# Reordering the engine queues of a fused linear-attention and FFN kernel: weight preparations, x's upper part, the last tiles' masks and y's parts

## The chip, the cores and the metric

The kernel runs on one core of one Trainium2 chip. The metric is the device time of one execution in microseconds (us). "PE" is TensorE, "DVE" VectorE, "ACT" ScalarE, "POOL" GpSimd and "SP" SyncE, whose queue starts every DMA of this kernel.

## What is computed

```python
x = L0_attn_x                                  # (8, 1024, 512) f32
x = x + attn(layernorm(x), W_attn, b_attn, W_proj, b_proj)
x = x + ffn(layernorm(x), weight, bias)
# attn: q, k, v = split(x @ W_attn + b_attn), 16 heads of 32
#       q, k = elu(q) + 1, elu(k) + 1
#       kv += k v^T; ksum += k, token by token (causal, linear attention)
#       y = (q kv) / (q ksum + 1e-6);  out = y @ W_proj + b_proj
# ffn:  e4m3(x) @ e4m3(weight).T + bias, operands rounded to fp8
```

## The kernel before

The 8192 tokens are cut into NT = 64 tiles of 128. Every engine runs its own hand-written list of steps in one loop over the tile number n, and semaphores alone tie the lists together; within a list nothing overtakes. So the order in which a helper is called in an engine's loop is the order in its queue, and a step whose semaphore is late holds all that stands behind it.

The work of tile n: TensorE makes the causal scores of two halves (`scores(n)`), VectorE multiplies them by a mask into `raw` (also called `scores(n)` on its list, "the mask" below), TensorE multiplies them, the queries and the running state by v (`values(n)`), VectorE divides (`values(n)`: `den`, then `y`). y is split into two f16 parts (ACT the upper, POOL the lower) and transposed by a DMA into `yt`. For the last four tiles (`tail(n)`, n = 60 to 63) TensorE transposes y (`t_y`), ACT copies the upper part (`s_yth`) and VectorE subtracts the lower one (`s_ytl`). One tile later TensorE projects (`proj(n)`: 12 matmuls, of which the last four alone read y's lower part), VectorE adds the result to x and takes the statistics of the second layer norm; POOL normalises (`proj(n)` on its list, into `x2`), ACT rounds to fp8 and bf16 (`t2`), a DMA transposes (`x2t`; for tiles 62 and 63 TensorE), and in the tile after that TensorE runs `ffn(n)`; ACT takes the result out (`o16`), VectorE adds it (`ffn`), and SP stores the rows.

For four tiles at a time TensorE makes twelve products ahead: eight "features" (q and k; `phi` on ACT and DVE turns each into `qk`) and four v. `chunks(n)` spreads them over the loop, three in each tile, the third behind the step `k_tokens`. The last tiles have none left. Products and transposes share four PSUM banks in a ring (`take`): the k-th waits until the (k-4)-th is emptied. `update(n)` on TensorE and VectorE moves the running state (`mid`, `state`), `spread` on ACT copies it into v, `queries` copies q (`raw<-qk`). `ln1` is the first layer norm eight tiles ahead: its upper f16 part is made by ACT and its lower by POOL (`ln1_parts`, `xnhl`), and SP starts a transposing DMA into `xt`.

W_proj is split into `wph` and `wpl` (`proj_weight`), the FFN weight is clipped and rounded to fp8 in steps (`ffn_low`, `ffn_high`, `ffn_round`, `ffn_sum`). SP's loop over n holds, in this order: the transposing of y(n-1), of x2(n-2), of x(n+8), in n = 1 the four of the FFN weight, the load of tile n+10 (for tiles 10 to 13 behind `s_wpl`, since their buffer holds W_proj first), and the store of tile n-2, which waits for VectorE's `ffn(n-2)`.

ACT's loop, which sets the steps of the tail, has this order:

```python
if n >= 2:
    t2(n - 2)
ahead(chunks(n)[0])
if tail(n - 1):
    t_y(n - 1)
if n + 1 < NT:
    k_tokens(n + 1)
```

Of the kernel before, what the change touches and what calls it, by code (L numbers as in the profile page):

```python
# [20 lines left out]
NT = B * T // P  # L21
# [4 lines left out]
NX = 14  # L26
# [23 lines left out]
def tail(n):  # L50
    return n >= NT - 4


def chunks(n):


    j, c = divmod(n, 4)
    if n < NT - 5:
        return [(j + 1, 3 * c), (j + 1, 3 * c + 1)], [(j + 1, 3 * c + 2)]
    return [(NB - 1, 9 + n - (NT - 5))] if n < NT - 2 else [], []  # L60
# [15 lines left out]
def build(nc, x_d, wa_d, ba_d, wp_d, bp_d, wf_d, bf_d, out_d):  # L76
    ctx = ExitStack()
    with ctx:
# [9 lines left out]
        xs = sb("xs", [P, NX, D], F32)  # L88
# [35 lines left out]
        st2 = sb("st2", [P, 4, 12], F32)  # L124
# [79 lines left out]
        def _(e):  # L204
# [13 lines left out]
            def matmul(out, a, b, start, stop):  # L218
                return e.matmul(out, a, b, start=start, stop=stop, skip_group_check=True)  # L219
# [116 lines left out]
            def proj(n):  # L336
                out = take(("proj", n), s_x1, n + 1)
                pe.wait_ge(s_wpl, 1)
                if tail(n):
                    pe.wait_ge(s_yth, n - NT + 5)  # L340
                    pe.wait_ge(s_ytl, n - NT + 5)
                else:
                    pe.wait_ge(s_yt[n % 2], 16 * (n // 2 + 1))
                mms = [(a + h, b, h) for a, b in ((0, wph), (0, wpl), (4, wph)) for h in range(4)]
                for i, (k, b, h) in enumerate(mms):
                    mm = matmul(out[:, :], yt[:, n % 2, k, :], b[:, h, :], i == 0, i == 11)
                mm.then_inc(s_proj, 1)

# [56 lines left out]
        def _(e):  # L405
# [45 lines left out]
            def ln1_parts(m):  # L451
                act.wait_ge(s_xn, m + 1)
                if m >= 8:
                    act.wait_ge(s_xt[m % 4], 16 * (m // 4 - 1))
                copy(xnhl[:, m % 4, 0, :], xn[:, m % 2, :]).then_inc(s_xhi, 1)
# [73 lines left out]
            def ahead(made):  # L529
                for j, s in made:  # L530
                    if s < 8:
                        phi(j, ORDER[s])
# [33 lines left out]
            for n in range(NT + 2):  # L566
                j, c = divmod(n, 4)
                if n < NT:
                    if n == 0:
                        spread(n)  # L570
                        proj_weight()
# [4 lines that stand above are left out]
                        t_y(n - 1)  # L576
                    if n + 1 < NT:
                        k_tokens(n + 1)
                    if n + 8 < NT:
                        ln1_parts(n + 8)  # L580
                    if n:
                        ahead(chunks(n)[1])
                    if n + 1 < NT:
                        queries(n + 1)
                    values(n)
                    if n == 0:
                        ahead(chunks(n)[1])
                if n == NT - 1:
                    t_y(n)
                if n >= NT:  # L590
                    t2(n - 2)
                if n >= 2:
                    ffn(n - 2)
                if n + 1 < NT:
                    spread(n + 1)

        @block.vector
        def _(e):
            dve = Engine(e)

            def stats(src, row, s_bn, s_var, n):
                e.bn_stats(row[:, 0:6], src).then_inc(s_bn, 1)  # L602
                dve.wait_ge(s_bn, 2 * n + 1)
                e.bn_aggr(row[:, 6:8], row[:, 0:6]).then_inc(s_bn, 1)  # L604
                dve.wait_ge(s_bn, 2 * n + 2)
                e.tensor_scalar(row[:, 8:9], row[:, 6:7], -1.0, None, ALU.mult)
                e.tensor_scalar(row[:, 9:10], row[:, 7:8], LN_EPS, None, ALU.add).then_inc(s_var, 1)  # L607
# [75 lines left out]
            def proj(n):  # L683
                x = xs[:, n % NX, :]
                dve.wait_ge(s_proj, n + 1)
                dve.wait_ge(s_xb, xb_count(n))
                e.scalar_tensor_tensor(x, bank["proj", n][:, :], UN_P, x, ALU.mult, ALU.add).then_inc(s_x1, 1)  # L687
                dve.wait_ge(s_x1, n + 1)
                if n >= 4:
                    dve.wait_ge(s_x2, n - 3)  # L690
                stats(x, st2[:, n % 4, :], s_bn2, s_var2, n)

            def ffn(n):
                x = xs[:, n % NX, :]
# [4 lines left out]
            def ahead(made):  # L699
                for j, s in made:  # L700
                    if s < 8:
                        phi(j, ORDER[s])
                    else:
                        v_out(j, s - 8)
# [72 lines left out]
            def ffn_high():  # L777

                dve.wait_ge(s_whi, 1)
                dve.wait_ge(s_wfd, 1)  # L780
                e.scalar_tensor_tensor(w_hi, w_hi, 2.0, w_lo, ALU.mult, ALU.subtract, saturate=False).then_inc(s_wfd, 1)
# [6 lines left out]
            def ffn_sum(first, end):  # L788
                dve.wait_ge(s_wfd, 3)
                for f in range(first, end):  # L790
                    e.tensor_tensor(w_b[:, f, :], w_hi[:, f, :], w_lo[:, f, :], ALU.add).then_inc(s_wfd, 1)
# [36 lines left out]
            update(0)  # L828
            proj_scale()
            for n in range(NT + 2):  # L830
                j, c = divmod(n, 4)
                if n < NT:
                    scores(n)
                    if n == 1:
                        ffn_sum(0, 2)
                    if n + 8 < NT:
                        ln1(n + 8)
                    if n == 0:
                        ffn_high()
                    ahead(chunks(n)[0][:1])  # L840
                    ahead(chunks(n)[0][1:])
                    if tail(n - 1):
                        t_y(n - 1)
                    if n:
                        ahead(chunks(n)[1])
                    values(n)
                    if n == 0:
                        ahead(chunks(n)[1])
                if 1 <= n <= NT:
                    proj(n - 1)  # L850
                if n + 1 < NT:
                    update(n + 1)
                if n == 0:
                    proj_weight()
                    ffn_round()
                if n == 1:
                    ffn_sum(2, 4)
                if n == NT - 1:
                    t_y(n)
                if n >= 2:  # L860
                    ffn(n - 2)

        @block.gpsimd
        def _(e):
# [80 lines left out]
            for n in range(NT + 1):  # L945
                if n < NT:
                    if n + 8 < NT:
                        ln1(n + 8)
                    if n + 8 < NT:
                        add_bp(n + 8)  # L950
                        ln1_parts(n + 8)
                    if n < 8:
                        add_bp(n)
                    values(n)
                if n >= 1:
                    proj(n - 1)
# [105 lines left out]
```

## Time and profile before

| | us |
|---|---|
| median of 3 runs (lowest to highest) | 989.68 (987.88 to 990.79) |
| profiled execution, its own time | 989.57 |
| span in the profile | 987.8 |
| TensorE busy | 951.9 (96%) |
| VectorE / ScalarE / GpSimd busy | 703.1 / 743.6 / 503.9 |
| mean granted TensorE clock | 0.990 |

The span runs from the first to the last instruction; 1.8 us of the execution's own time lie outside it. A granted clock of 1.00 is 2.4 GHz, 0.50 is 1.2 GHz. Busy time tells which engine is close to full; the waits tell where it stands still.

### The profile page before, as it was taken

To read this page: it belongs to the slowest core of one execution; us is meant where nothing else is said; L and a number is where in the kernel's file an instruction comes from. 1 tells how busy PE (TensorE), PEld (TensorE's weight loads), DVE (VectorE), ACT (ScalarE), POOL (GpSimd) and SP (SyncE) were. 2 spreads that over 40 slices of the span, in tenths; PEclk is the share of its full clock that TensorE was granted. 3 is DMA by queue.
4 is the path that set the end of the run, shared out by engine and by line. 5 is a ranking of instruction groups with operands and counts; after the bars stand their busy time and mean duration, and the time that the engine had idled before them with its cause. 6 is when DMAs were issued, how large, how long until landed. Compare 5 with 4: busy or idle time off the path is not lost.

```text
span 987.8 us, 44710 instructions
## 1 busy us (share of the span) xinstructions
PE 951.9 (96%) x19698; PEld 521.7 (53%) x19760; DVE 703.1 (71%) x1395; ACT 743.6 (75%) x1423; POOL 503.9 (51%) x521
## 2 busy tenths in 40 slices
PE   5998999999999999999999999999999999999985
PEld 2454555555555555555555555555555555555552
DVE  6977777676676777668677677767667676765674
ACT  5776686877878688787868868687786868777763
POOL 5536656555555455464555555555545546432323
PEclk9999999999999999999999999999999999999998
DMA  8824454544454434434335345454354453422311
GB/s 267 127 35 83 77 99 72 83 93 73 83 92 85 86 77 93 74 81 95 76 83 93 72 79 97 72 83 93 83 79 86 92 79 77 84 45 56 57 35 48
DMA packets 185362, 82.58 MB, mean 84 GB/s; under 512 B 165841, under 2 KB 165841, under 8 KB 185169
## 3 DMA queue, kind: packets, MB, share of 16 engines
q1 hardware_dynamic: 185168, 79.73, 42.6%
q8 instruction: 155, 2.54, 1.1%
q14 instruction: 39, 0.31, 0.1%
HBM read 22.81 MB, written 16.78 MB: 40 GB/s over the span
## 4 chain that ended last, share of the span: by engine, by line
PE 92%; DVE 4%; issue 1%; ACT 1%; POOL 1%; DMA 0%; POOLq 0%
PE R L219 76%; PE S L219 13%; PE R L223 3%; DVE raw L641 1%; POOL st L868 1%; DVE st L602 1%; POOL xn L870 0%; DVE xs L687 0%; DVE xs L697 0%; DMA xs<-in_L_attn_x 0%; ACT raw L409 0%; DVE v L630 0%; DVE wpl L769 0%; ACT wl L428 0%; DVE st L604 0%
## 5 line engine op out<-in xcount | busy, mean ns | idle before, releaser
L219 PE MATMUL R<-xt,wh 128*128 128x512 f16 x1024 | 306.8, 382 | 3.0 <-ACT wh L409 2.4
L409 ACT ACTIVATE raw<-qk 64x512 f32<-64x512 f32 x256 | 160.8, 628 | 76.8 <-PE S L219 73.8
L618 DVE SCALAR_TENSOR_TENSOR qk<-qk,rel 128x512 f32<-128x512 f32 x128 | 98.0, 768 | 149.8 <-ACT rel L421 145.3
L899 POOL TENSOR_TENSOR yhl<-y,yhl 128x512 f16<-128x512 f32 x60 | 69.5, 1159 | 255.8 <-ACT yhl L409 255.8
L219 PE MATMUL R<-xt,wl 128*128 128x512 f16 x512 | 194.2, 380 | 0.0
L868 POOL TENSOR_TENSOR st<-st,half 128x1 f32<-128x1 f32 x128 | 74.8, 584 | 168.3 <-DVE st L607 166.9
L219 PE MATMUL R<-wh,xt 128*128 128x512 f16 x512 | 160.3, 379 | 0.0
L641 DVE TENSOR_TENSOR raw<-S,causal 64x1024 f32<-64x1024 f32 x128 | 155.9, 1218 | 0.9
L219 PEld LDWEIGHTS R<-xt,wh 128*128 128x128 f16 x1024 | 96.8, 98 | 110.7 <-DVE xt L735 2.6
L418 ACT ACTIVATE qk<-R,bqk,wm 128x512 f32<-128x512 f32 x128 | 98.9, 772 | 61.4 <-PE R L219 61.3
L219 PE MATMUL R<-wph,yt 128*128 128x512 f16 x512 | 134.2, 385 | 2.0 <-DVE yt L680 2.0
L630 DVE SCALAR_TENSOR_TENSOR v<-R,wm,bv 64x512 f32<-64x512 f32 x128 | 96.0, 750 | 25.9 <-PE R L219 24.0
L421 ACT ACTIVATE rel<-R,bqk,wm 128x512 f32<-128x512 f32 x128 | 98.6, 770 | 2.3 <-DVE qk L618 2.3
L219 PEld LDWEIGHTS S<-v,raw 128*32 128x32 f32 x8192 | 79.3, 110 | 33.9 <-issue 26.5
L219 PE MATMUL R<-wl,xt 128*128 128x512 f16 x256 | 97.0, 379 | 0.0
L219 PE MATMUL S<-v,raw 128*32 128x33 f32 x8192 | 86.7, 199 | 7.8 <-DVE raw L641 5.9
L602 DVE BATCH_NORM_STATS2 st<-xs 128x6 f32<-128x512 f32 x128 | 88.8, 694 | 6.3 <-DMA xs<-in_L_attn_x 2.3
L687 DVE SCALAR_TENSOR_TENSOR xs<-R,wm,xs 128x512 f32<-128x512 f32 x64 | 48.0, 750 | 63.5 <-PE R L219 63.5
L885 POOL TENSOR_TENSOR xnhl<-xn,xnhl 128x512 f16<-128x512 f32 x60 | 70.1, 1169 | 29.4 <-ACT xnhl L409 29.4
L908 POOL TENSOR_TENSOR xs<-xs,bf 128x512 f32<-128x512 f32 x64 | 82.0, 1281 | 5.3
L892 POOL TENSOR_TENSOR xs<-xs,bp 128x512 f32<-128x512 f32 x64 | 82.2, 1284 | 4.7
L409 ACT ACTIVATE v<-mid 32x132 f32<-32x132 f32 x256 | 80.3, 314 | 3.8 <-DVE mid L652 0.9
(88 smaller groups left out, 1330.0 us busy)
## 6 DMA issues: line engine op xcount, KB each, us to landing
xs<-in_L_attn_x SPq DMA_DIRECT2D x64, 256.0 KB, 3.7
out<-xs SPq DMA_DIRECT2D x64, 256.0 KB, 2.3
raw<-in_L_attn_W_attn SPq DMA_DIRECT2D x3, 1024.0 KB, 10.6
xs<-in_L_attn_W_proj SPq DMA_DIRECT2D x4, 256.0 KB
raw<-in_L_ffn_weight SPq DMA_DIRECT2D x1, 1024.0 KB, 17.6
x2t<-x2b SPq DMA_TRANSPOSE x62, 2.4
xt<-xnhl SPq DMA_TRANSPOSE x60, 4.1
yt<-yhl SPq DMA_TRANSPOSE x60, 3.3
```

Source lines behind the costliest of these rows:

```text
L219: return e.matmul(out, a, b, start=start, stop=stop, skip_group_check=True)
L409: return e.activation(out, in_, ACT.Copy, **more)
L418: e.activation(dst[:, i, :], bank["qkv", j, i][:, :], ACT.Exp, scale=UN[i // 4], bias=bqk[:, i:i + 1])
L421: e.activation(rel[:, u % 2, :], bank["qkv", j, i][:, :], ACT.Relu, scale=UN[i // 4], bias=bqk[:, i:i + 1]).then_inc(s_relu, 1)
L602: e.bn_stats(row[:, 0:6], src).then_inc(s_bn, 1)
L618: e.scalar_tensor_tensor(qk[j % 2][:, i, :], qk[j % 2][:, i, :], 1.0, rel[:, (u - 1) % 2, :], ALU.min, ALU.add).then_inc(s_phi, 1)
L630: made = e.scalar_tensor_tensor(v1[rows, n % NV, a, :, 0:32], heads(bank["qkv", j, 8 + t][rows, :]), UN_V[rows], heads(bv[rows, :]), ALU.m ...
L641: made = e.tensor_tensor(dst, scored(a), causal_over(a), ALU.mult)
L868: e.tensor_tensor(row[:, 10:11], row[:, 9:10], half[:, :], ALU.pow).then_inc(s_rs, 1)
L885: e.tensor_tensor(xnhl[:, m % 4, 1, :], xn[:, m % 2, :], xnhl[:, m % 4, 0, :], ALU.subtract).then_inc(s_xlo, 1)
L892: e.tensor_tensor(x, x, bp[:, :], ALU.add).then_inc(s_xb, 1)
L908: e.tensor_tensor(x, x, bf[:, :], ALU.add).then_inc(s_x1b, 1)
```

## The change

Nothing is computed differently; instructions change places in three queues, and one wait moves.

- VectorE: `proj_weight` (wpl) goes ahead of tile 0's features, `ffn_high` and `ffn_round` behind tile 0's y; `ffn_sum(0, 2)` behind `ln1(9)`. The statistics of the second layer norm become a step of their own (`ln2`). For tiles 58 to 61 they, and `ffn` of the tile before, are called one iteration later, behind the mask of tiles 60 to 63. In n = 63 `t_y(63)` comes ahead of `ln2(62)`.
- ScalarE: x's upper part (`ln1_parts`) is made behind the third product of the tile instead of ahead of it. GpSimd: `add_bp(n)` of the first eight tiles goes ahead of `ln1_parts(n + 8)`.
- TensorE: in the tail's `proj` the wait for y's lower part stands ahead of the ninth matmul instead of the first.

```diff
 def proj(n):                       # TensorE
     if tail(n):
         pe.wait_ge(s_yth, n - NT + 5)
-        pe.wait_ge(s_ytl, n - NT + 5)
...
     for i, (k, b, h) in enumerate(mms):
+        if tail(n) and i == 8:
+            pe.wait_ge(s_ytl, n - NT + 5)
         mm = matmul(out[:, :], yt[:, n % 2, k, :], b[:, h, :], i == 0, i == 11)
...
 # ScalarE's loop
         k_tokens(n + 1)
-    if n + 8 < NT:
-        ln1_parts(n + 8)
     if n:
         ahead(chunks(n)[1])
+        if n + 8 < NT:
+            ln1_parts(n + 8)
...
     if n == 0:
         ahead(chunks(n)[1])
+        ln1_parts(n + 8)
...
 # VectorE
     e.scalar_tensor_tensor(x, bank["proj", n][:, :], UN_P, x, ALU.mult, ALU.add).then_inc(s_x1, 1)
+
+def ln2(n):
     dve.wait_ge(s_x1, n + 1)
     if n >= 4:
         dve.wait_ge(s_x2, n - 3)
-    stats(x, st2[:, n % 4, :], s_bn2, s_var2, n)
+    stats(xs[:, n % NX, :], st2[:, n % 4, :], s_bn2, s_var2, n)
...
         scores(n)
+        if tail(n):
+
+            ln2(n - 2)
+            ffn(n - 3)
...
     if 1 <= n <= NT:
         proj(n - 1)
+    if n == NT - 1:
+        t_y(n)
+    if 1 <= n <= NT and not NT - 4 <= n + 1 < NT:
+        ln2(n - 1)
     if n + 1 < NT:
         update(n + 1)
-    if n == 0:
-        proj_weight()
-        ffn_round()
...
-    if n >= 2:
+    if n >= 2 and not NT - 4 <= n + 1 < NT:
         ffn(n - 2)
...
 # GpSimd's loop
         add_bp(n + 8)
-        ln1_parts(n + 8)
     if n < 8:
         add_bp(n)
+    if n + 8 < NT:
+        ln1_parts(n + 8)
```

VectorE's queue from tile 0's `ln1(8)` to the mask of tile 1, before (`wpl<-xs` is `proj_weight`; `raw<-raw` with 2048 elements is `ffn_high`, then `ffn_round`; `raw<-S` the mask). Line numbers of the changed kernel are two to four higher for the same step.

```order
L781 SCALAR_TENSOR_TENSOR raw<-raw 128x2048
L618 SCALAR_TENSOR_TENSOR qk1<-qk1,rel 128x512 x2
L666 TENSOR_SCALAR den<-S 128x16
L668 RECIPROCAL den<-den 128x16
L676 TENSOR_TENSOR y<-S,den 128x512
L618 SCALAR_TENSOR_TENSOR qk1<-qk1,rel 128x512
L652 TENSOR_TENSOR mid<-R3,state 128x132
L655 TENSOR_TENSOR state<-R0,mid 128x132
L769 SCALAR_TENSOR_TENSOR wpl<-xs,wm,wph 128x2048
L785 TENSOR_SCALAR raw<-raw 128x2048
L641 TENSOR_TENSOR raw<-S,causal 64x4x256 x2
```

The same stretch of VectorE's queue in the changed kernel:

```order
L773 SCALAR_TENSOR_TENSOR wpl<-xs,wm,wph 128x2048
L620 SCALAR_TENSOR_TENSOR qk1<-qk1,rel 128x512 x2
L668 TENSOR_SCALAR den<-S 128x16
L670 RECIPROCAL den<-den 128x16
L678 TENSOR_TENSOR y<-S,den 128x512
L785 SCALAR_TENSOR_TENSOR raw<-raw 128x2048
L789 TENSOR_SCALAR raw<-raw 128x2048
L620 SCALAR_TENSOR_TENSOR qk1<-qk1,rel 128x512
L654 TENSOR_TENSOR mid<-R3,state 128x132
L657 TENSOR_TENSOR state<-R0,mid 128x132
L643 TENSOR_TENSOR raw<-S,causal 64x4x256 x2
```

wpl has taken the place of `ffn_high`, and both steps on the FFN weight stand between y(0) and tile 0's third feature; nothing of the weights is left between `state` and tile 1's mask.

VectorE's queue in the tail, from proj(58)'s addition to x (`xs<-R3`) to v of the next tiles, before (`st2` are the statistics of tile 58, `xs<-o16` is ffn(57), `raw<-S` the mask of tile 60):

```order
L687 SCALAR_TENSOR_TENSOR xs<-R3,wm,xs 128x512
L602 BN_STATS st2<-xs 128x6
L604 BN_AGGR st2<-st2 128x2
L606 TENSOR_SCALAR st2<-st2 128x1
L607 TENSOR_SCALAR st2<-st2 128x1
L652 TENSOR_TENSOR mid<-R1,state 128x132
L655 TENSOR_TENSOR state<-R2,mid 128x132
L697 TENSOR_TENSOR xs<-o16,xs 128x512
L641 TENSOR_TENSOR raw<-S,causal 64x4x256 x2
L630 SCALAR_TENSOR_TENSOR v1<-R3,wm,bv 64x16x32 x2
```

The same stretch in the changed kernel:

```order
L689 SCALAR_TENSOR_TENSOR xs<-R3,wm,xs 128x512
L654 TENSOR_TENSOR mid<-R1,state 128x132
L657 TENSOR_TENSOR state<-R2,mid 128x132
L643 TENSOR_TENSOR raw<-S,causal 64x4x256 x2
L604 BN_STATS st2<-xs 128x6
L606 BN_AGGR st2<-st2 128x2
L608 TENSOR_SCALAR st2<-st2 128x1
L609 TENSOR_SCALAR st2<-st2 128x1
L701 TENSOR_TENSOR xs<-o16,xs 128x512
L632 SCALAR_TENSOR_TENSOR v1<-R3,wm,bv 64x16x32 x2
```

The mask has gone from behind the statistics and ffn to ahead of both; the same happens in the next three tiles.

ScalarE's queue in n = 62, which reads the same before and after (`x28`, `x2b` are t2(60), made of POOL's normalised tile 60; `yt` is the upper part of y(61), `ktok` belongs to update(63), `raw<-qk1` are the queries of tile 63):

```order
L410 ACTIVATE x28<-x2 128x512
L410 ACTIVATE x2b<-x28 128x512
L410 ACTIVATE yt<-R0 128x512
L410 ACTIVATE ktok<-R1 128x512
L410 ACTIVATE raw<-qk1 64x2x256 x4
```

Nothing moved there: t2(60) still stands ahead of the upper part of y(61).

## Rows read from the trace of the kernel before

**Rows 1.** TensorE's waits from 50 us on (us in total, times, longest)

```profile
PE S L219 <- DVE raw L641: 5.9, 3, 2.5
PE S L219 <- DVE y L676: 3.8, 1, 3.8
...
PE S L219 <- issue: 1.9, 1, 1.9
...
PE R L219 <- ACT rel L421: 0.6, 1, 0.6
```

**Rows 2.** Windows, a steady one and one behind a long wait (busy, PEclk)

```profile
500.00:600.00 100.00, 99.50 (x2133) 54.50 (x2138) 72.31 (x144) 76.39 (x151) 52.89 (x54) 1.00 0.46 83
...
82.00:86.00 4.00, 3.88 (x73) 2.17 (x74) 3.86 (x11) 3.54 (x10) 2.75 (x3) 0.63 0.89 110
```

**Rows 3.** Timeline of VectorE, 57 to 74 us (start, us, line, op)

```profile
57.18 2.28 DVE L781 SCALAR_TENSOR_TENSOR raw<-raw 128x2048 fp8e4<-128x2048 fp8e4 x1
...
66.57 0.69 DVE L618 SCALAR_TENSOR_TENSOR qk<-qk,rel 128x512 f32<-128x512 f32 x1 [4.68 <-ACT rel L421]
...
67.71 2.34 DVE L769 SCALAR_TENSOR_TENSOR wpl<-xs,wm,wph 128x2048 f16<-128x2048 f32 x1
69.97 1.22 DVE L785 TENSOR_SCALAR raw<-raw 128x2048 fp8e4<-128x2048 fp8e4 x1
```

**Rows 4.** Timeline of TensorE, 70 to 84 us

```profile
73.61 1.30 PE L219 MATMUL S<-v,raw 128*32 128x33 f32 x128 [1.23 <-DVE raw L641]
...
82.12 1.28 PE L219 MATMUL S<-qk 32*64 32x64 f32 x64 [3.83 <-DVE y L676]
```

**Rows 5.** Timeline of GpSimd and SP's queue, 57 to 71 us

```profile
57.35 2.52 POOL L868 TENSOR_TENSOR st<-st,half 128x1 f32<-128x1 f32 x1 [13.51 <-DVE st L607]
...
65.28 1.16 POOL L899 TENSOR_TENSOR yhl<-y,yhl 128x512 f16<-128x512 f32 x1 [0.27 <-ACT yhl L409]
...
70.48 1.24 SPq L982 DMA_TRANSPOSE yt<-yhl  x1
```

**Rows 6.** SP's queue, yt's landing times (915 us on) and TensorE, tile 60

```profile
928.81 0.34 SPq L1036 DMA_DIRECT2D out<-xs  x1
929.24 1.29 SPq L982 DMA_TRANSPOSE yt<-yhl  x1
...
DMA to landing us min/median/max: 3.0/4.0/5.0
...
934.66 1.69 PE L219 MATMUL R<-wph,yt 128*128 128x512 f16 x4
```

**Rows 7.** Timeline of VectorE, GpSimd and ScalarE, tiles 60 to 62

```profile
950.58 0.69 DVE L602 BATCH_NORM_STATS2 st<-xs 128x6 f32<-128x512 f32 x1
...
952.79 2.45 DVE L641 TENSOR_TENSOR raw<-S,causal 64x1024 f32<-64x1024 f32 x2
...
951.82 0.55 POOL L868 TENSOR_TENSOR st<-st,half 128x1 f32<-128x1 f32 x1 [7.60 <-DVE st L607]
952.47 1.04 POOL L870 TENSOR_SCALAR x<-xs,st 128x512 f32<-128x512 f32 x1
...
953.89 0.63 ACT L409 ACTIVATE x<-x 128x512 fp8e4<-128x512 f32 x1
...
955.09 0.58 ACT L409 ACTIVATE yt<-R 128x512 f16<-128x512 f32 x1
```

**Rows 8.** Timeline of TensorE, tiles 61 to 63 and the end

```profile
947.01 1.02 PE L219 MATMUL R<-wph,yt 128*128 128x512 f16 x4 [0.58 <-DVE yt L680]
...
951.24 0.91 PE L219 MATMUL S<-qk 32*64 32x64 f32 x64
...
961.91 0.91 PE L219 MATMUL S<-qk 32*64 32x64 f32 x64
...
971.03 0.60 PE L223 MATMUL R<-ident,y 128*128 128x128 f32 x4
...
980.29 0.63 PE L223 MATMUL R<-ident,x 128*128 128x128 f32 x4 [0.81 <-POOL x L870]
```

More of the change, by code:

```diff
@@ L830, in _ @@
             for n in range(NT + 2):
-                j, c = divmod(n, 4)
                 if n < NT:
                     scores(n)
-                    if n == 1:
-                        ffn_sum(0, 2)
+                    if tail(n):
+                        ln2(n - 2)
+                        ffn(n - 3)
                     if n + 8 < NT:
@@ L838, in _ @@
                     if n == 0:
-                        ffn_high()
-                    ahead(chunks(n)[0][:1])
-                    ahead(chunks(n)[0][1:])
+                        proj_weight()
+                    if n == 1:
+                        ffn_sum(0, 2)
+                    ahead(chunks(n)[0])
                     if tail(n - 1):
@@ L847, in _ @@
                     if n == 0:
+                        ffn_high()
+                        ffn_round()
                         ahead(chunks(n)[1])
@@ L850, in _ @@
                     proj(n - 1)
+                if n == NT - 1:
+                    t_y(n)
+                if 1 <= n <= NT and not NT - 4 <= n + 1 < NT:
+                    ln2(n - 1)
                 if n + 1 < NT:
                     update(n + 1)
-                if n == 0:
-                    proj_weight()
-                    ffn_round()
                 if n == 1:
                     ffn_sum(2, 4)
-                if n == NT - 1:
-                    t_y(n)
-                if n >= 2:
+                if n >= 2 and not NT - 4 <= n + 1 < NT:
                     ffn(n - 2)
```

## The prediction, made before the changed kernel ran

> **What bounds the kernel now.** I read the busy time by stretches first. In the steady part TensorE is busy for 99.5 of 100 us at the full clock [rows 2], with VectorE and ScalarE below 77 and GpSimd at 53. There an order is worth something only if it makes TensorE wait. Then the list of TensorE's waits from 50 us on [rows 1]: three waits for the mask (5.9 us), one for y (3.8), one for a feature (0.6), and 1.9 us put down to "issue". In the timeline they lie at two places: at tiles 0 to 2, and in the last four tiles, where no products made ahead fill the gaps. So two places are costed; the 57 tiles between are asked only whether they stay hidden. The granted clock is 0.63 in the 4 us from scores(2) on, which follow the 3.8 us wait [rows 2, 4]; the reader is to see that a long wait is paid for twice.
>
> **The head: what goes.** VectorE stands idle for 4.68 us between y(0) and tile 0's third feature, because ScalarE holds that feature back behind x's upper part and the queries; right behind it come wpl (2.34 us) and ffn_round (1.22), and only then the mask of tile 1 [rows 3]. The change puts wpl where ffn_high was (2.34 against 2.28 us, no matter) and ffn_high and ffn_round (2.28 + 1.22 = 3.5 us) into the idle 4.68. ScalarE's feature also comes about 0.6 us earlier. So tile 1's mask comes some 4.6 us earlier, and the 0.6 us wait for the feature [rows 1] and the 1.23 us wait for tile 1's mask, ahead of its values [rows 4], are gone. y(1) also loses x(9)'s path through VectorE, GpSimd and ScalarE ahead of its last feature, so it gains more, about 7 us; scores(2) moves up only by TensorE's own three waits, 0.6 + 1.2 + 3.8 = 5.7 us (to about 76.4, y(1) being ready near 75), and the slow clock behind the long wait goes with it: 4.0 us at 0.63 lose at most 1.5 us, I take 1.4. That is -7.1 us.
>
> **The head: what comes.** GpSimd's tiny power op took 2.52 us at 57.35, while VectorE ran ffn_high from 57.18 to 59.46 [rows 3, 5]; the same op takes 0.55 elsewhere [rows 7]. So ffn_high, in its new place, holds GpSimd for up to 2.3 us, and ffn_round perhaps for another 1.2, at 62 to 65.5 us, where GpSimd now has two additions of the projection's bias, x(8)'s lower part (itself later, since its upper part is made some 3 us later) and then y(0)'s lower part, which ended at 66.44 before. Undisturbed I put it at 67.1, held for the full 3.5 us at 70.3. SP issued y(0)'s transposing at 70.48 although y was ready 4 us before: it stood behind the load of tile 10, which waits for wpl; that wait is over at 59.5 now. proj(0) began 1.2 us behind the start of the values at 73.61 [rows 4], so it will want yt at 74.8 - 0.6 - 1.2 = 73.0. Undisturbed, issue at 67.7 and a landing of 3.0 to 5.0 us [rows 6] give at the latest 72.7: no wait. Held for 3.5 us, issue at 70.9 gives 73.9 to 75.9: 0.9 to 2.9 us. I take 1.2 us; bounds 0 and 2.9. The Trainium skill (GPSIMD Engine Reference, section 8, Key points) says that GpSimd shares its SBUF interfaces with VectorE and contends with VectorE's instructions that have two SBUF inputs or run in a 2-port mode. The trace agrees for ffn_high; whether the one-input ffn_round counts no row shows. If it does in full, this term would be about 2.0 instead of 1.2 by that page, if the page did not hold at all, 0. The head comes to -7.1 + 1.2 = -5.9 us (-7.1 to -4.2).
>
> **The middle: nothing.** ScalarE's later upper part of x delays x's transposing by 2 to 3 us in two tiles of four; it is made eight tiles ahead, and in the two tiles whose third product is v the order is as before. GpSimd's lower part of x then ends well before y's, for which it waits anyway. If that cover failed, TensorE would wait at each group of four tiles; nothing in 99.5 of 100 us points to it.
>
> **The tail, tile 60.** SP's store of tile 57 waits for VectorE's ffn(57), and the transposing of y(59) stands right behind it (928.81, 929.24 [rows 6]). ffn(57) now comes behind the mask (2.45 us) and the statistics (1.2): SP is released 3.5 us later, at 932.7 for y(59). With the 4.0 us landing of the row proj(59) can begin at 936.8, against 934.66: +2.1 (landing 3.0 to 5.0: +1.1 to +3.1). The 1.9 us of "issue" lie just ahead of 934.66, within tile 60's values; they lie under the new wait, so their absence would give nothing back.
>
> **The tail, tiles 61 to 63.** Let T be the start of scores(n) on TensorE. Before, T advances by 961.91 - 951.24 = 10.7 us a tile [rows 8]. In the changed kernel the chain is: scores 0.9, then the mask 2.45, then the statistics of tile n-2 and GpSimd's normalising, 950.58 to 953.51 = 2.9 us, then ScalarE's t2(n-2) and, right behind it, the upper part of y(n-1), 953.89 to 955.67 = 1.8 [rows 7]; with the handovers proj(n-1) begins at T + 8.3. TensorE has nothing else: its next instruction is that proj. Before, the statistics were two steps ahead of the mask, and y's copy was there in time. From proj to the next scores are 951.24 - 947.01 = 4.2 us at full clock [rows 8]; behind a wait of 2.5 us or more I add the same 1.4 for the slow clock (0 to 1.5); behind the 1.9 us pause four matmuls took 1.69 us, without a wait of that length 1.02 [rows 6, 8]. T advances by 8.3 + 4.2 + 1.4 = 13.9, that is +3.3 us, for 61 to 62 and for 62 to 63. From scores(63) to t_y(63) it was 971.03 - 961.91 = 9.1; now 8.3 + 2.7 + 1.4 = 12.4: +3.3. What the earlier mask saves (0.6 us a tile, since the mask then waits for scores itself) is inside: values run earlier, and then TensorE waits at proj. The ninth matmul's later wait is worth nothing here: y's lower part is 0.7 us behind the upper, and eight matmuls take 1.7.
>
> **The end.** With t_y(63) ahead of the statistics, and proj free to begin on y's upper part, proj(63) begins about 1.4 us earlier after its transposes. But the last transposes of x (980.29 [rows 8], 9.3 us behind t_y(63)) also wait for tile 62 to pass: transposes 0.6, copy 0.6, y's lower part 0.7, statistics and normalising 2.9, transposes 0.6, two copies 1.3, ffn 1.0, handovers 0.4: 8.1 us. That is -1.2.
>
> The tail: +2.1 + 3.3 + 3.3 + 3.3 - 1.2 = +10.8 us. **The sum:** -5.9 + 10.8 = +4.9 on the profiled execution's own 989.57 us, so 994.5; the median of the runs shown, 989.68, is 0.1 away, which changes nothing.
>
> **Rivals.** (A) Forecast: 994.5, chance 0.50. (B) The clock keeps its level through the new waits and GpSimd is not held: head -7.1, tail 10.8 - 3 x 1.4 = 6.6, so 989.1, within 0.3%. For it: after the 1.23 us wait 128 small matmuls took only 1.30 us [rows 4]; against it: the new waits are longer than that, and behind 1.9 and 3.8 us the matmuls were slow [rows 2, 6]. With halfway cases 0.26. (C) Faster: t2(n-2) is not what y's copy stands behind. Then each mask is 0.6 us earlier, the slow stretches of tiles 62 and 63 go (1.4 each), the end gives 1.2: tail -(1.2 + 2.8 + 1.2) = -5.2, head -7.1, 977.3. It is decided by one thing: whether normalised tile n-2 reaches ScalarE before the transposed y(n-1) does; the queue puts it first, and the statistics come 4 us later than they did, so I give it 0.08. (D) Worse: GpSimd's full hold and a slow stretch behind it (head -4.2 + 1.4 = -2.8), a landing of 5.0 us (tail 11.8), and the "issue" pause falling on a bare stretch (1.9 + 1.4): 989.57 - 2.8 + 11.8 + 3.3 = 1001.9; with halfway cases 0.16.
>
> **Numbers.** What a measurement of this kernel can tell from no change is 0.3%, 3.0 us: 986.7 to 992.7. Faster is C, 0.08. Within 0.3% is B, 0.26. Slower is A and D, 0.66. The range takes in the bounds of the head, the landing and the clock: from -7.1 + 6.6 (989.1, cut at 989.0) to -4.2 + 11.8 and one slow stretch of 1.4 more (998.6, cut at 998.5).
>
> **What would show it.** Right: scores(2) at 76 to 78 us; a wait of 0 to 3 us at proj(0); a wait of about 2 us or more for yt at proj(59), with SP's y(59) behind its store; three waits of TensorE for ScalarE's yt in tiles 61 to 63, the clock at half behind them, scores 13 to 14 us apart; t_y(63) to the end about 1 us shorter. Wrong: masks of tiles 62 and 63 still what TensorE waits for, or ScalarE's copies of y where they were.

## The result: 1.2% slower, and why the sum missed it

The changed kernel took 1001.55 us (median of 4 runs, 998.51 to 1002.24) against 990.05 (987.88 to 990.79) before: a ratio of 1.0123, 95% interval 1.0103 to 1.0143. The prediction was 994.5 us with a range of 989.0 to 998.5. The direction was right; the size was not, and the time lies outside the range. Executions of one kernel differ by about 2 us with the granted clock: of the 44 runs of the kernel before that the experiments were set beside, the 16 with a mean clock of 0.993 or more took 987.2 us in the mean and the others 989.4.

The profile after: a span of 1000.5 us, a mean granted clock of 0.987. TensorE's waits from 50 us on, the counterpart of [rows 1]:

```profile
PE R L219 <- ACT yt L410: 9.9, 3, 3.7
PE R L219 <- DMA yt<-yhl: 7.1, 3, 3.5
PE S L219 <- DVE raw L643: 3.5, 2, 2.0
...
PE S L219 <- issue: 1.4, 2, 1.0
```

The three waits of the tail for ScalarE's yt were forecast. Of the 7.1 us for transposed y, 3.2 lie at proj(59), as forecast, 0.3 at proj(0), and 3.5 at a place that the prediction doesn't mention: proj(1).

To see where the time goes I set the start of each scores(n) on TensorE beside that of the kernel before. scores(0) comes 0.7 us later already, ahead of anything that was changed, so the head is counted from there.

| | after minus before, us | forecast |
|---|---|---|
| scores(0) | +0.72 | |
| scores(2), against scores(0) | -4.6 | -5.7 |
| scores(3), against scores(0) | -0.4 | -5.9 |
| scores(3) to scores(60) | +1.0 | 0 |
| scores(60) to (61), to (62), to (63) | +3.1, +3.7, +3.2 | +2.1, +3.3, +3.3 |
| scores(63) to t_y(63), and from there to the end | +3.3, -1.8 | +3.3, -1.2 |

The last two lines of the table come to +11.4 (before rounding), forecast +10.8. The head's gain is there at scores(2) and gone one tile later. TensorE at proj(0), scores(2) and proj(1) after the change (columns as in [rows 4]):

```profile
74.44 1.02 PE L219 MATMUL R<-wph,yt 128*128 128x512 f16 x4 [0.33 <-DMA yt<-yhl]
...
78.23 0.91 PE L219 MATMUL S<-qk 32*64 32x64 f32 x64 [0.35 <-DVE y L678]
87.39 1.44 PE L219 MATMUL S<-v,raw 128*32 128x33 f32 x128
92.32 1.02 PE L219 MATMUL R<-wph,yt 128*128 128x512 f16 x4 [3.50 <-DMA yt<-yhl]
93.18 1.56 PE L219 MATMUL R<-wpl,yt 128*128 128x512 f16 x4
94.54 1.91 PE L219 MATMUL R<-wph,yt 128*128 128x512 f16 x4
```

proj(1) could start at 88.8 and waits until 92.3 for y(1); the groups of four matmuls behind it take 1.56 and 1.91 us instead of 1.03, and the granted clock is 0.69 in the window of 92 to 96 us (columns as in [rows 2]; the clock is the third number from the end):

```profile
92.00:96.00 4.00, 3.68 (x12) 1.52 (x13) 0.00 (x0) 0.56 (x1) 1.51 (x2) 0.69 0.57 132
```

Here is proj(1) before, without a wait:

```profile
93.67 1.04 PE L219 MATMUL R<-wph,yt 128*128 128x512 f16 x4
```

SP's queue shows why. First before, then after the change (the wft rows are the four transposes of the FFN weight, the last yt is y(1)):

```profile
80.33 1.23 SPq L974 DMA_TRANSPOSE xt<-xnhl  x1
81.60 5.97 SPq L1030 DMA_TRANSPOSE wft<-raw  x4
87.62 0.58 SPq L967 DMA_DIRECT2D xs<-in_L_attn_x  x1
88.25 1.24 SPq L982 DMA_TRANSPOSE yt<-yhl  x1
```

```profile
70.75 1.24 SPq L990 DMA_TRANSPOSE yt<-yhl  x1
80.47 1.23 SPq L982 DMA_TRANSPOSE xt<-xnhl  x1
81.75 5.20 SPq L1038 DMA_TRANSPOSE wft<-raw  x4
86.99 0.58 SPq L975 DMA_DIRECT2D xs<-in_L_attn_x  x1
87.62 1.23 SPq L990 DMA_TRANSPOSE yt<-yhl  x1
```

y(1) is ready some 4 us earlier (scores(2), which waited for it in both, moved from 82.12 to 78.23), but its transpose is issued only 0.6 us earlier, and TensorE has it 4.7 us after that, at 92.3. Before, it was in time: the trace puts the landing 3.5 us behind the issue, at 88.25 + 3.5 = 91.8, against a proj(1) that began at 93.67, a slack of 1.9 us that no list of waits shows. Now proj(1) could start 4.9 us earlier (88.8), and the landing is 0.5 us later, since the transpose took 1.1 us longer: 4.9 - 1.9 + 0.5 = 3.5 us of wait. Why it took longer is open.

### The profile page after: what moved, and what is told of

The parts are those of the page before. It is cut to its first block, busy times and chain, and to the rows that moved or that the text cites. A ratio compares the mean times of both kernels' runs of the same rounds, so it can differ in the third digit from the quotient of the medians.

```text
span 1000.5 us, 44771 instructions
## 1 busy us (share of the span) xinstructions
PE 958.9 (96%) x19760; PEld 521.7 (52%) x19760; DVE 712.4 (71%) x1395; ACT 740.3 (74%) x1423; POOL 519.4 (52%) x521
## 4 chain that ended last, share of the span: by engine, by line
PE 90%; DVE 4%; issue 2%; POOL 2%; DMA 1%; ACT 1%; SPq 1%; ACTq 0%; POOLq 0%
PE R L219 75%; PE S L219 12%; PE R L223 3%; DVE raw L643 1%; DMA yt<-yhl 1%; POOL st L875 1%; DVE st L604 1%; SPq L1038 0%; POOL xn L877 0%; ACT x L410 0%; POOL x L877 0%; DVE raw L785 0%; DVE qk L620 0%; DMA xs<-in_L_attn_x 0%; ACT yt L410 0%
## 5 line engine op out<-in xcount | busy, mean ns | idle before, releaser
L620 DVE SCALAR_TENSOR_TENSOR qk<-qk,rel 128x512 f32<-128x512 f32 x128 | 104.0, 815 | 140.2 <-ACT rel L422 138.8
L875 POOL TENSOR_TENSOR st<-st,half 128x1 f32<-128x1 f32 x128 | 89.2, 697 | 161.0 <-DVE st L609 160.7
L219 PE MATMUL R<-wph,yt 128*128 128x512 f16 x512 | 137.1, 392 | 17.0 <-ACT yt L410 9.9
L604 DVE BATCH_NORM_STATS2 st<-xs 128x6 f32<-128x512 f32 x128 | 88.8, 694 | 6.4 <-DMA xs<-in_L_attn_x 2.5
L899 POOL TENSOR_TENSOR xs<-xs,bp 128x512 f32<-128x512 f32 x64 | 84.7, 1328 | 4.7
```

The lines of the kernel that those rows point to most:

```text
L620: e.scalar_tensor_tensor(qk[j % 2][:, i, :], qk[j % 2][:, i, :], 1.0, rel[:, (u - 1) % 2, :], ALU.min, ALU.add).then_inc(s_phi, 1)
L875: e.tensor_tensor(row[:, 10:11], row[:, 9:10], half[:, :], ALU.pow).then_inc(s_rs, 1)
L899: e.tensor_tensor(x, x, bp[:, :], ALU.add).then_inc(s_xb, 1)
```

## Why x(9)'s transpose did not come earlier

SP's y(1) stands behind x(9)'s transpose, and that waits for GpSimd. VectorE (first fence) and GpSimd (second), after the change, 62 to 81 us:

```profile
62.59 3.02 DVE L785 SCALAR_TENSOR_TENSOR raw<-raw 128x2048 fp8e4<-128x2048 fp8e4 x1
65.64 2.17 DVE L789 TENSOR_SCALAR raw<-raw 128x2048 fp8e4<-128x2048 fp8e4 x1
67.73 1.64 DVE L620 SCALAR_TENSOR_TENSOR qk<-qk,rel 128x512 f32<-128x512 f32 x1
...
69.82 2.45 DVE L643 TENSOR_TENSOR raw<-S,causal 64x1024 f32<-64x1024 f32 x2
```

```profile
62.17 4.55 POOL L899 TENSOR_TENSOR xs<-xs,bp 128x512 f32<-128x512 f32 x2
66.69 2.13 POOL L892 TENSOR_TENSOR xnhl<-xn,xnhl 128x512 f16<-128x512 f32 x1
68.78 1.60 POOL L906 TENSOR_TENSOR yhl<-y,yhl 128x512 f16<-128x512 f32 x1
73.54 0.93 POOL L875 TENSOR_TENSOR st<-st,half 128x1 f32<-128x1 f32 x1 [3.15 <-DVE st L609]
74.57 1.85 POOL L877 TENSOR_SCALAR xn<-xs,st 128x512 f32<-128x512 f32 x1
76.50 2.82 POOL L899 TENSOR_TENSOR xs<-xs,bp 128x512 f32<-128x512 f32 x2
79.29 1.15 POOL L892 TENSOR_TENSOR xnhl<-xn,xnhl 128x512 f16<-128x512 f32 x1
```

Before, the same steps of VectorE took 2.28, 1.22 and 0.69 us [rows 3], and one addition on GpSimd 1.28. Now both engines are slower: each takes its own time plus the wait for the other's instruction. GpSimd's first addition runs from 62.17 to 63.45; ffn_high, begun at 62.59, gets its 2.28 us behind it and ends at 65.6; the second addition, held meanwhile, ends at 66.7; ffn_round, begun at 65.64, gets its 1.22 us behind that and ends at 67.8; and so on in turn to y(0)'s lower part. Each sum comes out 0.1 to 0.2 us above its row. Had the two engines shared evenly while both were at work, ffn_high would have ended at 67.0 (an estimate from the same lengths), not at 65.6. The Trainium skill (Trainium Architecture — The Big Picture, What this means for kernel authors) calls the port pair that VectorE and GpSimd share "an exclusive lock (not a bandwidth split)"; the trace agrees, and a lock costs both sides. The prediction charged GpSimd alone.

x(9)'s statistics do reach GpSimd 2.5 us earlier (73.54; before 76.03). Then its normalising takes 1.85 us instead of 0.77, and two additions of the bias (2.82) stand ahead of x(9)'s lower part instead of one (1.27): 1.1 + 1.5 = 2.6 us, all of the 2.5. GpSimd's rows before:

```profile
77.07 0.77 POOL L870 TENSOR_SCALAR xn<-xs,st 128x512 f32<-128x512 f32 x1
77.92 1.27 POOL L892 TENSOR_TENSOR xs<-xs,bp 128x512 f32<-128x512 f32 x1
79.14 1.16 POOL L885 TENSOR_TENSOR xnhl<-xn,xnhl 128x512 f16<-128x512 f32 x1
```

## The experiments

"The end's edits" are the later wait for y's lower part in proj(60) to proj(63), and t_y(63) ahead of the statistics of tile 62. scores(0), which lies ahead of every edit, starts between 0.35 us earlier and 0.84 us later than in the profile of before, so profiles are compared from scores(0) on. The medians of the kernel before were 988.5 to 989.2 in these runs and 990.05 in the result above, so a ratio says more than a difference of medians.

**1. The changed kernel with the tail's late statistics put back.**

```diff
         scores(n)
-        if tail(n):
-            ln2(n - 2)
-            ffn(n - 3)
...
-    if 1 <= n <= NT and not NT - 4 <= n + 1 < NT:
+    if 1 <= n <= NT:
         ln2(n - 1)
...
-    if n >= 2 and not NT - 4 <= n + 1 < NT:
+    if n >= 2:
         ffn(n - 2)
```

> The changed kernel with ln2 and ffn of tiles 57 to 61 back where they were on VectorE (the later wait for y's lower part and t_y(63) ahead of the statistics stay). Theory A (the whole loss is the late statistics of the last tiles; the head gives back what it gains): the profile's tail loses its +11.4 us up to scores(63) and t_y(63) but keeps the shorter end, so 988 to 989.5 us, that is the kernel before less 0.4 (head) and 1 to 1.8 (end); no wait of TensorE for ScalarE's yt over 1 us, none for y(59)'s DMA. Rival B (the reordered head, with its 3.5 us wait at proj(1), carries a large part of the loss): 994 us or more.

Measured: 985.66 us, ratio 0.9973 (0.9959 to 0.9987), 2.8 us under its reference, where theory A's terms came to 1.4 to 2.2. All of the loss is in this part. The wait at proj(1) is still there (3.4 us): scores(3) starts 0.7 us earlier, against scores(0), scores(2) 4.6.

**2. The kernel before with the late statistics alone.** It is the opposite edit, with the statistics as a step of their own:

```diff
         scores(n)
+        if tail(n):
+            ln2(n - 2)
+            ffn(n - 3)
```

> The kernel before with only ln2 and ffn of tiles 57 to 61 moved behind the masks of tiles 60 to 63. Theory A: the loss of the tail by itself, +11 to +13 us (1001 to 1003): +3.1 at tile 60, +3.7 and +3.2 for scores 61 to 62 and 62 to 63, +3.3 to t_y(63), without the end's gain. Rival B (the loss needs the head's edits too): under +6 us. The head must read as in the kernel before: scores(2) near 82, no wait at proj(1).

Measured: 1006.9 us, ratio 1.0184 (1.0163 to 1.0204): above the 1003 of theory A, and worse than the changed kernel. TensorE's waits from 50 us on name the lower part of y now:

```profile
PE R L219 <- DVE yt L680: 13.7, 4, 4.4
```

So the ninth matmul's later wait, forecast as worth nothing, pays for part of the late statistics.

**3. The changed kernel with ScalarE's t2(n-2) behind y's upper part and the keys.**

```diff
-    if n >= 2:
+    if n >= 2 and not tail(n - 1):
         t2(n - 2)
...
     if n + 1 < NT:
         k_tokens(n + 1)
+    if tail(n - 1):
+        t2(n - 2)
```

> The changed kernel with ScalarE's t2(n-2) put behind y's upper part and k_tokens in n = 61 to 63. Theory A1 (the queue on ScalarE is what makes proj wait): the three waits for yt (9.9 us) go; proj(n-1) starts at about T + 4.7 to 6, and ffn(n-2) then waits for x2t, which still lands at T + 10 to 12, so scores(61) to scores(62) take about 12.5 us instead of 14.35: 995 to 997 us in all. Rival A2 (the late statistics themselves bind; the order on ScalarE only chooses which matmuls wait): the wait moves whole to ffn(n-2), and no more than 1 us is gained: 1000 to 1001.5.

Measured: 995.95 us, ratio 1.0074 (1.0052 to 1.0096): theory A1. ScalarE no longer stands idle in front of y's copy; x's rounding follows it:

```profile
947.10 0.60 ACT L410 ACTIVATE yt<-R 128x512 f16<-128x512 f32 x1 [1.45 <-PE R L223]
947.60 0.60 ACT L410 ACTIVATE ktok<-R 128x512 f32<-128x512 f32 x1
949.53 0.63 ACT L410 ACTIVATE x<-x 128x512 fp8e4<-128x512 f32 x1 [1.34 <-POOL x L879]
```

In the changed kernel GpSimd's and ScalarE's rows of the same tile are:

```profile
949.68 0.93 POOL L875 TENSOR_TENSOR st<-st,half 128x1 f32<-128x1 f32 x1 [13.38 <-DVE st L609]
950.71 0.77 POOL L877 TENSOR_SCALAR x<-xs,st 128x512 f32<-128x512 f32 x1
...
951.51 0.63 ACT L410 ACTIVATE x<-x 128x512 fp8e4<-128x512 f32 x1 [3.89 <-POOL x L877]
952.17 0.63 ACT L410 ACTIVATE x2b<-x 128x512 bf16<-128x512 fp8e4 x1
952.71 0.58 ACT L410 ACTIVATE yt<-R 128x512 f16<-128x512 f32 x1
```

There ScalarE is idle for 3.89 us, in the last 2.5 of which the transposed y lies ready (its transposes run from 948.45 to 949.05), behind the head of ScalarE's queue. But x2 now comes late to ffn, and TensorE waits there instead, 5.9 us in three waits:

```profile
PE R L219 <- DMA x2t<-x2b: 5.9, 3, 2.9
```

**4. The changed kernel with SP's store of tile 57 behind y(59)'s transpose.**

```diff
     if 1 <= n <= NT:
         t_y(n - 1)
+    if n == NT - 4:
+        store(n - 3)
...
-    if n >= 2:
+    if n >= 2 and n != NT - 5:
         store(n - 2)
```

> The changed kernel with the store of tile 57 behind the transposing of y(59) on SP's queue (one place). Theory A (the store waits for the late ffn(57) and holds y(59)): y(59) is issued at about 929 instead of 934.1, the 3.2 us wait at proj(59) goes, ffn(58) waits up to 2.5 us for x2t(58) instead, and 2 to 3.5 us are gained: 998 to 999.5 us. Rival (y(59) lands late for another reason, or x2t(58) takes all of it over): within 0.5 us of the changed kernel, 1001 to 1002.

Measured: 999.81 us, ratio 1.0115 (1.0095 to 1.0136). The wait at proj(59) is gone, and the twelve matmuls of proj(59) run at the full clock: from scores(60) to (61) 1.4 us are gained on the kernel before, where the changed kernel loses 3.1. The next tile loses 5.4 instead of 3.7, so a part is waited for again. The profile is 3.4 us shorter than the changed kernel's, the medians differ by 1.7, between theory A and the rival, and the two ratios differ by 0.8 us, with intervals that overlap. So the cause of the wait at proj(59) is shown; what its removal is worth in this kernel is not resolved.

**5. The edits of experiments 3 and 4 together.**

> The changed kernel with two moves in the last tiles together: ScalarE's additions to x for t2(n-2) stand behind y's and ktok's work for n = 61, 62 and 63 (alone: 995.95 us), and SP's store of tile 57 stands behind y(59)'s transpose (alone: 999.81). Theory S (the two waits are separate terms of the sum, 9.9 us at proj(60) to proj(62) behind ScalarE and 3.2 us at proj(59) behind the store): the gains add, 992.5 to 994.5 us, with no wait of 1 us or more at proj(59). Rival T (the time saved at proj(59) is waited for again at proj(60), because y(60) hangs on VectorE's chain and not on TensorE): 995 to 996.5 us.

Measured: 992.47 us, ratio 1.0051 (1.0036 to 1.0067). The gains add, theory S, and with 1.7 us to spare: by medians 5.6 and 1.7 us alone, 9.1 together. It is still slower than before: late statistics leave waits for x2t (5.8 us in five).

**6. The first experiment's kernel, with SP's FFN weight transposes split around y(1).** It is the one that tests the head.

```diff
     if 1 <= n <= NT:
         t_y(n - 1)
+    if n == 1:
+        ffn_weight(0, 2)
+    if n == 2:
+        ffn_weight(2, 4)
     if n >= 2:
         t2(n - 2)
     if n + 8 < NT:
         t1(n + 8)
-    if n == 1:
-        for f in range(4):
-            sp.wait_ge(s_wfd, 4 + f)
-            e.dma_start(wft[:, :, f * P:(f + 1) * P], w_b[:, f, :], transpose=True).then_inc(s_wft, 16)
```

> The kernel is the changed one with its last tiles as before (that is the run with the tail put back, 985.66 us), and with SP's transposes of feature(0) split: the first two are issued right behind y(0), ahead of t1(9), the last two right behind y(1)'s transpose. Theory Q (what gives the head's gain back is SP's queue, in which y(1)'s transpose stands behind t1(9) and four transposes of feature(0) that end at 86.6 us, so that y(1) lands about 92 while TensorE is ready for proj(1) at 88.8): y(1)'s transpose is issued at 81 to 83 us, the wait of 3.4 us at proj(1) goes, and with it the slow clock behind it (1 to 1.7 us): 980 to 982 us, scores(3) starts 4 to 5 us earlier than in the run with the tail put back. Rival R (y(1) itself is late, or ffn(0) takes up the wait because the last two transposes of feature(0) are later): a wait of 2 to 3 us at the first layer ffn(0) or at proj(1) stays, and the time is within 1 us of 985.7.

Measured: 978.99 us, ratio 0.9921 (0.9894 to 0.9948), 6.7 us under experiment 1. SP's queue and proj(1) on TensorE:

```profile
74.21 3.23 SPq L999 DMA_TRANSPOSE wft<-raw  x2
80.60 1.23 SPq L978 DMA_TRANSPOSE xt<-xnhl  x1
81.88 0.58 SPq L971 DMA_DIRECT2D xs<-in_L_attn_x  x1
82.50 1.24 SPq L986 DMA_TRANSPOSE yt<-yhl  x1
83.78 2.58 SPq L999 DMA_TRANSPOSE wft<-raw  x2
```

```profile
88.77 1.04 PE L219 MATMUL R<-wph,yt 128*128 128x512 f16 x4
89.64 1.03 PE L219 MATMUL R<-wpl,yt 128*128 128x512 f16 x4
```

No wait at proj(1), no slow group behind it, and x(9)'s transpose still where it was: the place of the four transposes is enough to hold y(1) back. scores(3) starts 5.7 us earlier than before, against scores(0); the forecast for the whole head was 5.9. Theory Q. The time is 1 us under the 980 to 982 that it gave: against experiment 1 scores(3) comes 5.1 us earlier, and the two profiles differ by 2.0 us more at tile 60, where the program is the same: the matmuls of proj(59) take 1.03 us a group here, and 1.33, 1.91 and 1.62 there.

**7. The first experiment's kernel, with GpSimd's `add_bp(n)` back behind `ln1_parts(n + 8)`.** `add_bp(n + 8)` stays ahead of it, as in the kernel before, so one addition of two moves, where the expectation speaks of both.

> The kernel is the changed one with its last tiles as before, and with GpSimd's additions of bp(8) and bp(9) and their two partner rows put back behind ln1_parts(8) and ln1_parts(9). Theory Q (SP's queue behind t1(9) sets y(1)'s landing): x's lower part for tile 9 is ready 1.4 to 2.8 us earlier, SP's whole chain moves with it, and the wait of 3.4 us at proj(1) falls to 1 to 2 us: 983.5 to 984.5 us against the 985.66 of the run with the tail put back. Rival R (the landing of y(1) doesn't hang on GpSimd's order): the wait at proj(1) stays at 3 us or more and the time is within 0.7 us of 985.7.

Measured: 983.64 us, ratio 0.9955 (0.9942 to 0.9968). A miss for theory Q's numbers: the wait at proj(1) is 3.3 us (3.4 in experiment 1). SP issued x(9)'s transpose 1.2 us earlier, against scores(0), but that issue took 1.93 us instead of 1.23, and y(1)'s came only 0.5 earlier and took 0.6 us longer to be used (5.2 us). The profile shows no gain (scores(3) at -0.5 us against -0.7 in experiment 1), the median shows 2.0 us, and the two intervals overlap. Whether this edit is worth anything is open.

**8. The first experiment's kernel, with GpSimd's additions last in n = 0 and 1.**

```diff
-    if n + 8 < NT:
+    if n + 8 < NT and n >= 2:
         add_bp(n + 8)
-    if n < 8:
+    if 2 <= n < 8:
         add_bp(n)
     if n + 8 < NT:
         ln1_parts(n + 8)
     values(n)
+    if n < 2:
+        add_bp(n + 8)
+        add_bp(n)
```

> The kernel is the changed one with its last tiles as before, and for n=0 and n=1 both additions of bp stand last in GpSimd's row, behind ln1_parts(n+8) and behind y's lower part, so that GpSimd has nothing to do beside VectorE's round and ffn_high of tile 0's weights. Theory M (VectorE's and GpSimd's operations lengthen each other when they run together, 3.02 for 2.28, 2.17 for 1.22 and 1.64 for 0.69 us on VectorE): ffn_high falls to about 2.3, the round to 1.2, the feature's part to 0.7 us, mask(1) comes 2 to 2.5 us earlier, t1(9) is issued at 76.5 to 78 and y(1)'s transpose at 83.5 to 85; the wait at proj(1) falls to 0 to 1.5 us: 981 to 983.5 us. Rival N (these operations are long for another reason, for instance what they read): their durations stay within 0.2 us of 3.02, 2.17 and 1.64, and the time within 1.5 us of 984.5.

Measured: 981.35 us, ratio 0.9934 (0.9908 to 0.9959). VectorE's rows:

```profile
62.04 2.28 DVE L785 SCALAR_TENSOR_TENSOR raw<-raw 128x2048 fp8e4<-128x2048 fp8e4 x1
64.35 1.23 DVE L789 TENSOR_SCALAR raw<-raw 128x2048 fp8e4<-128x2048 fp8e4 x1
65.50 1.64 DVE L620 SCALAR_TENSOR_TENSOR qk<-qk,rel 128x512 f32<-128x512 f32 x1
```

The two weight steps have their old lengths. GpSimd has nothing beside ffn_high; x(8)'s lower part begins at 64.73, behind the start of ffn_round, and is the one held, 1.86 us instead of 1.16. The feature starts beside that part and stays at 1.64, against the expected 0.7. So the length follows what GpSimd has already begun, not what VectorE reads, for the one-input ffn_round too. Rival N falls. y(1)'s transpose is issued at 84.17, the wait at proj(1) falls to 2.4 us (0 to 1.5 was expected, since 5.2 us passed from its issue to its use), and scores(3) starts 3.0 us earlier.

**9. Experiments 6 and 8 in one kernel.**

> The kernel is the changed one with its last tiles as before, with SP's transposes of feature(0) split around y(1)'s (alone: 978.99 us) and with both additions of bp last in GpSimd's row for n=0 and n=1 (alone: 981.35 us). Theory M (VectorE and GpSimd lengthen each other's operations around tile 0, and once y(1) is in time VectorE's way to mask(1) sets scores(2) and all behind it): scores(2) starts 5.5 to 6.5 us before that of the kernel before, measured against scores(0), scores(3) 6.5 to 7.5 us before, and the time is 976.5 to 978 us. Rival T (proj(0), that is y(0)'s landing, takes up what VectorE gains): scores(3) stays within 0.5 us of the split alone, and so does the time, 978.5 to 979.5 us.

Measured: 978.27 us, ratio 0.9897 (0.9880 to 0.9914). It is the fastest version found, 1.0% under the kernel before. scores(2) starts 5.9 us earlier, as expected; scores(3) only 6.2 (6.5 to 7.5 was expected), 0.4 more than in experiment 6, as rival T had it, and the two medians can't be told apart. Theory M's gain at scores(2) is there, and its gain in time is not. From 74 to 106 us TensorE waits for nothing longer than 0.33 us, so there is little left to win in that stretch.

**10. The kernel before with the end's edits alone.**

```diff
         pe.wait_ge(s_yth, n - NT + 5)
-        pe.wait_ge(s_ytl, n - NT + 5)
...
+        if tail(n) and i == 8:
+            pe.wait_ge(s_ytl, n - NT + 5)
...
+    if n == NT - 1:
+        t_y(n)
     if 1 <= n <= NT:
         ln2(n - 1)
```

> The kernel is the one before with two small parts of the change alone: TensorE waits for the lower part of y ahead of the ninth matmul of proj(60) to proj(63) instead of ahead of the first, and VectorE writes the parts of y(63) ahead of the statistics of tile 62. Theory E (the prediction's term for the end, 1.2 us, where the run with the tail put back showed an end that is 1.6 us shorter): 1.0 to 1.8 us are gained behind t_y(63) and none ahead of it, 986.9 to 987.7 us against 988.5. Rival W (the ninth matmul's later wait gains at proj(60) to proj(62) in the order of before too): 1.5 to 3 us more, 984 to 985.5 us.

Measured: 985.56 us, ratio 0.9969 (0.9958 to 0.9980): 3.6 us under its reference, near rival W. The waits of 0.58 us [rows 8] and 1.43 us for VectorE's yt are gone; 0.6 us are gained from scores(61) to scores(62) and 1.8 behind t_y(63). The profile gains another 1.3 us from scores(62) to scores(63), where the 2.1 us wait for a mask has no slow group behind it (1.43 us in the first fence, 1.96 before in the second, both for the same 128 matmuls), and 2.0 at tile 60. These two can't be put down to the edits: experiment 7 has the same steps in its last tiles and took 1.99 us there, and the edits begin only behind tile 60's matmuls. So the waits alone are worth about 2.4 of the 3.6 us:

```profile
953.45 1.43 PE L219 MATMUL S<-v,raw 128*32 128x33 f32 x128 [2.12 <-DVE raw L642]
954.82 1.04 PE L219 MATMUL R<-wph,yt 128*128 128x512 f16 x4
```

```profile
955.29 1.96 PE L219 MATMUL S<-v,raw 128*32 128x33 f32 x128 [2.11 <-DVE raw L641]
957.18 1.82 PE L219 MATMUL R<-wph,yt 128*128 128x512 f16 x4
```

**11. The changed kernel with the wait for y's lower part ahead of the first matmul again.**

> The changed kernel with one part undone: TensorE waits for the lower part of y ahead of the first matmul of proj(60) to proj(63) again, instead of ahead of the ninth. Theory L (behind the late statistics the upper part of y is the last thing that proj waits for, and the lower part comes 0.7 to 1.2 us after it, so that the later wait hides it in three or four tiles): proj waits for the lower part, 4.4 us each for three tiles, and the time is 2 to 4.5 us over the changed kernel's 1001.55, 1003.5 to 1006 us. Rival N (the later wait is worth nothing there, as forecast): within 1 us of 1001.55.

Measured: 1004.46 us, ratio 1.0160 (1.0143 to 1.0177), 2.9 us over the changed kernel. proj waits for the lower part for 3.4, 4.4 and 4.4 us, then 0.64 at proj(63). Theory L.

## Why the prediction was wrong

**The head: what goes: nearly right.** The waits for tile 0's feature and tile 1's mask are gone, the one for y is 0.35 us (forecast 0). scores(2) came at 78.23 us, outside the 76.4 that the text gave and just beyond its 76 to 78, since 0.33 us of wait at proj(0), 0.36 for `mid` and 0.35 for y were left, 1.0 of the 5.7, and scores(0) was 0.7 late. The mask of tile 1 came 2.0 us earlier against scores(0), not 4.6, and y(1) 4.6, not 7, since VectorE's two weight steps and the feature took 2.6 us longer beside GpSimd; that was nearly enough, as TensorE needed only 1.8 and 5.7. Experiment 6, with y(1)'s transpose in time, shows 4.6 us at scores(2) and 1.1 for the clock (forecast 5.7 and 1.4).

**The head: what comes: the step that failed.** It followed y(0) through SP's queue and put +1.2 us at proj(0), bounds 0 and 2.9. It measured 0.33 there, though GpSimd was held in full, by ffn_round too: y(0)'s lower part ended at 70.38 (forecast 70.3 for the full hold) and its transpose was issued at 70.75 (70.9), but landed 3.6 us later, and proj(0) itself was ready only at 74.1, not at 73.0. The text did not follow y(1), for which "The head: what goes" had only y's own gain of 7 us. The cost was 3.5 us of wait at proj(1), and 1.8 of slow clock behind it (5.3 in all between scores(3) of experiment 6 and of the changed kernel). The sum could be made from the trace of before: y(1)'s transpose issued at 88.25 behind 6 us of FFN weight transposes and landed at 91.8, proj(1) at 93.67; TensorE 5 us earlier, SP not. That gives some 3 us of wait; the 1.1 us by which the transpose took longer are in no row of before. The head's result was -0.4, not -5.9: these 5.5 us, 0.7 that were there at scores(0), 1.0 of small drifts in the middle and 0.6 in the tail are the 7.8 between the profiled span's +12.7 and the forecast's +4.9. Experiment 1 against 10 says the same without a profile: with or without the head's edits the time is 0.9973 and 0.9969 of the kernel before.

**The middle: nothing: right.** No wait for an engine or a DMA appears between 110 and 918 us, only two of 0.4 us put down to "issue". The drift here is made of steps of up to 0.6 us, and most such steps lie at other tiles in other executions; between scores(4) and scores(60) it is +1.1 us here and -0.4 to +0.9 in the experiments' kernels.

**The tail, tile 60: right place, price a little low.** Against scores(60), proj(59) began 2.2 us later (938.18 after 3.23 us of wait, 4.1 us behind its transpose's issue), as forecast. The other 0.9 of the +3.1 is a slow stretch that is longer than the one before: all twelve matmuls of proj(59) took 1.87 to 1.91 us a group, where the last group had taken 1.26. Experiment 4 shows that the wait comes from SP's store: with the store behind y(59) it is gone.

**The tail, tiles 61 to 63: right.** The chain ran as written: mask at 945.95, statistics, GpSimd, ScalarE's t2 and then yt, proj(60) at 953.43 after 2.72 us of wait, 8.4 us behind scores(61) (forecast 8.3); scores 14.35 and 13.82 us apart (forecast 13.9). Experiment 3 shows that t2(n-2) ahead of y's copy is the cause.

**"The ninth matmul's later wait is worth nothing here": wrong, though the sum does not suffer by it.** The chain let proj(n-1) begin on y's upper part, at T + 8.3, and so had the later wait inside; 8.4 was measured. With the wait back in its old place proj waits for the lower part, 0.7 to 0.9 us more in each of three tiles and 0.64 at proj(63) (experiment 11, 2.9 us by medians). So the late statistics with the old wait cost 18 us (experiment 2), and the text's 12.0 is to be set beside the changed kernel's 3.1 + 3.7 + 3.2 + 3.3 = 13.3.

**The end: right place, size too small.** -1.8 for -1.2, and -1.8 to -1.9 in every other profile with both of the end's edits and the statistics in their old place. The last transposes of x come 7.9 us behind t_y(63) (forecast 8.1, before 9.3); the rest is the last ffn at the full clock, 1.02 us instead of 1.58. In the tail, then, three terms were too small by 1.0, 0.4 and 0.6 us, the last of them a gain: 11.4 for 10.8 is a sum whose terms hold, with a little luck in the signs.

**The rivals.** B (the clock keeps its level) fell: behind the four long waits of the tail the first four matmuls took 1.65 to 1.87 us. C fell with the masks: ScalarE's queue does put t2 first. D named the nearest time, 1001.9, and that is luck: GpSimd's full hold came true but cost 0.33 us at proj(0), y(59) was used 4.1 us behind its issue, not 5.0, and no "issue" pause fell on a bare stretch of 3.3 us.

## What to carry to other kernels

When an order makes one engine 5 us earlier at some point, list everything that it takes from other queues in the next two tiles, with the slack that each had. A transfer that was in time by 1.9 us appears in no list of waits, and behind a queue that doesn't move it takes the whole gain back. Then move the queue as well: here the gain was real and was had for a change of place in SP's list. And put no urgent copy behind a step whose input has just been made later; if both are needed, count which of them TensorE reads first.

## What was not expected of the hardware

- VectorE and GpSimd took turns instruction by instruction: 3.02, 2.17 and 1.64 us on VectorE for 2.28, 1.22 and 0.69, and 4.55 us on GpSimd for two additions of 1.28. A one-input fp8 `TENSOR_SCALAR` on VectorE (1.23 us alone, 2.17 beside an addition) takes part.
- Transposed y(1) was used 4.6 to 5.2 us after its issue in every kernel where proj(1) waited for it, at the top of the 3.0 to 5.0 of [rows 6], where the kernel before had it in 3.5; SP needed 1.3 to 1.6 us to issue each transpose of the FFN weight, so the four in a row are 5.2 to 6 us of its queue.
- The granted clock is not a function of the wait alone. Behind the same 2.12 us wait for the mask of tile 62 the 128 matmuls took 1.43 us in experiment 10 and 1.99 in experiment 7, whose last tiles have the same steps. About 2 us of a difference between two profiles can be this alone.
